# Cross attention and mixture of experts in one kernel: the first group's products, banks and splits, two context roundings moved, the slot table in two loads

## What is computed

```
x = x + (fp8(layernorm(x)) @ fp8(ctx) + mask)          # per batch, one scale for each tensor
n = layernorm(x)
scores = sigmoid(n @ router_w.T)                       # best 3 of 8 groups, best 4 experts of those
slots: 160 per expert, filled in token order           # more are dropped
routed = (silu(Xp @ W_gate) * (Xp @ W_up)) @ W_down * weight, added to its token's row
shared = silu(n @ shared_gate.T) * (n @ shared_up.T) @ shared_down.T
out = x + routed + shared
```

## Time and profile before

| | us |
|---|---|
| median of 3 runs | 1987.12 (1985.38 to 1987.95) |
| profiled execution | 1987.5 |
| its span | 1985.9 |
| PE / DVE / ACT / POOL busy | 1831.9 / 1390.6 / 864.7 / 606.0 |
| mean granted clock of PE | 0.991 |

### The profile page before, as it was taken

How to read it: one execution, slowest core, us unless ns; L and a number is a source line. 1 busy time by engine, 2 the same in 40 slices (tenths; PEclk the granted TensorE clock), 3 DMA queues, 4 the chain that set the end, 5 groups by cost and what they waited for, 6 DMA issues and landing times.

```text
span 1985.9 us, 44057 instructions
## 1 busy us (share of the span) xinstructions
PE 1831.9 (92%) x17396; PEld 1398.4 (70%) x17396; DVE 1390.6 (70%) x2509; ACT 864.7 (44%) x1209; POOL 606.0 (31%) x611
## 2 busy tenths in 40 slices
PE   0039999999999999999999999999999999999997
PEld 0018578668667767766866876778888888888886
DVE  5888675576567557557545544588888888888884
ACT  8564221222212212122221121367777777777773
POOL 2100210220220221122022022355655656656552
PEclk9989999999999999999999999999999999999999
DMA  9936534433433443434243244499999999999993
GB/s 377 392 98 198 127 86 96 109 95 86 107 98 75 107 118 68 114 96 95 76 107 75 54 107 125 140 333 356 354 370 356 355 371 354 359 372 349 363 371 78
DMA packets 188301, 395.45 MB, mean 199 GB/s; under 512 B 116304, under 2 KB 120432, under 8 KB 163600
## 3 DMA queue, kind: packets, MB, share of 16 engines
q1 hardware_dynamic: 163184, 334.77, 49.0%
q0 software_dynamic: 23808, 58.81, 13.5%
q10 hardware_dynamic: 1184, 0.15, 0.0%
HBM read 314.79 MB, written 55.35 MB: 186 GB/s over the span
## 4 chain that ended last, share of the span: by engine, by line
PE 84%; issue 3%; DVE 2%; DMA 1%; POOL 1%; SPq 0%; ACT 0%; POOLq 0%; DVEq 0%; ACTq 0%
PE ps L1345 51%; PE ps L1358 15%; PE ps L1531 8%; PE ps L1385 5%; PE ps L1539 2%; PE ps L1421 1%; DVE W L1024 1%; PE ps L1451 1%; DMA xn_rows<-FR 1%; POOL slots L555 1%; DMA FR<-xn_rows,gix 0%; PE ps L1426 0%; PE ps L1457 0%; DMA BIG<-in_sh_down 0%; SPq L467 0%
## 5 line engine op out<-in xcount | busy, mean ns | idle before, releaser
L1345 PE MATMUL ps<-XT,W 128*128 128x256 f16 (+1 forms) x12288 | 1112.4, 253 | 5.0 <-issue 2.5
L1345 PEld LDWEIGHTS ps<-XT,W 128*128 128x128 f16 x12288 | 1025.0, 98 | 90.2 <-issue 15.4
L1289 DVE SCALAR_TENSOR_TENSOR W<-BIG,W 128x2048 f16<-128x2048 f32 x192 | 436.2, 2286 | 64.5 <-ACT W L848 64.5
L848 ACT ACTIVATE W<-BIG 128x2048 f16<-128x2048 f32 x192 | 361.4, 1901 | 0.0
L1358 PE MATMUL ps<-W,HH 128*128 128x512 f16 x1536 | 334.3, 379 | 0.0
L790 ACT ACTIVATE SG<-ps 128x256 f32<-128x256 f32 x128 | 48.9, 382 | 612.5 <-PE ps L1345 612.5
L1358 PEld LDWEIGHTS ps<-W,HH 128*128 128x128 f16 x1536 | 150.3, 98 | 180.8
L257 POOL TENSOR_TENSOR expo<-expo 128x1 f32<-128x1 f32 x159 | 82.1, 516 | 621.2 <-ACT FR L719 267.4
L1203 DVE SCALAR_TENSOR_TENSOR SG<-ps,SG 128x256 f32<-128x256 f32 x128 | 54.3, 424 | 232.7 <-ACT SG L790 232.7
L548 POOL TENSOR_TENSOR rs<-ve,expo 128x1 f32<-128x1 f32 x32 | 17.6, 549 | 565.0 <-DVE ve L1045 565.0
L599 POOL DMA_INDIRECT FR<-xn_rows,gix x64 | 173.0, 2703 | 30.0 <-issue 30.0
(11 more groups left out here) (178 smaller groups left out, 1627.7 us busy)
## 6 DMA issues: line engine op xcount, KB each, us to landing
BIG<-in_w_gate SPq DMA_DIRECT2D x64, 1024.0 KB, 9.0
BIG<-in_w_up SPq DMA_DIRECT2D x64, 1024.0 KB, 7.6
BIG<-in_w_down SPq DMA_DIRECT2D x64, 1024.0 KB, 8.2
X<-in_x SPq DMA_DIRECT2D x16, 1024.0 KB, 5.2
X<-in_mask POOLq DMA_DIRECT2D x16, 1024.0 KB, 8.1
xn_rows<-FR SPq DMA_DIRECT2D x32, 512.0 KB, 3.7
out_rows<-X SPq DMA_DIRECT2D x32, 512.0 KB, 3.6
W<-in_x SPq DMA_DIRECT2D x6, 2048.0 KB, 19.6
```

What stands on the lines that cost most here:

```text
L848: ac.activation(dst, stage, ACT.Copy, scale=W_SCALE).then_inc(x_hi, 1)
L1289: ve.scalar_tensor_tensor(out=lo[cut], in0=src, scalar=W_SCALE, in1=hi[cut], op0=ALU.mult, op1=ALU.subtract).then_inc(x_lo, 1)
L1345: ins = te.matmul(out_ps, a[:, k, cols], b[:, k, :], start=n == 0, stop=n == len(steps) - 1)
```

## The change

Group 0: the products of ic 0 and 1 become `first_products`: high weights against both parts of x, in halves of 128 tokens, then the low weights piece by piece. The second tile's transposes use banks 2 and 3 and the cross product's second tile banks 6 and 7 (4 and 5 the first time). DVE makes all low splits after the x transposes; the splits get two lists, one for ACT, one for DVE, the latter after h. The router's steps on DVE come one ic later. The down pieces have four stage buffers. Two context roundings move from the end of group 0 to ic 0 and 2 of group 1. The slot table is loaded for two experts, then for the rest. In the last expert the tail rows come first and are scattered by themselves, then each half. The diff, cut to its core (some indentation removed):

```diff
@@ -157,7 +158,7 @@
 sw_stage = [W[:, 32768 + 4096 * s:32768 + 4096 * (s + 1)].bitcast(F32) for s in range(4)]
-sd_stage = [BIG[:, 10240 + 2048 * s:10240 + 2048 * (s + 1)].bitcast(F32) for s in range(3)]
+sd_stage = [BIG[:, at:at + 2048].bitcast(F32) for at in (10240, 12288, 14336, 20480)]
@@ -280,7 +283,8 @@ orders of the splits
 SW_PIECES += [(2, k, 2, nh) for nh in range(2) for k in (0, 2, 4, 6)]
-FIRST_SPLITS = [(4, 5), (6,), (7,), (8,), (9,), (10,), (11, 12), (13, 14), (15,)]
+FIRST_HI = [(4, 5), (6,), (7,), (8, 9), (10,), (11,), (), (), (12, 13, 14, 15)]
+FIRST_LO = [(4,), (5,), (6, 7), (), (), (), (), (8, 9, 10, 11), (12, 13), (14, 15)]
@@ -303,11 +307,20 @@
 def sw_slot(n):
-  return (n % 4, sw_stage[n % 4]) if n < 8 else (4 + (n - 8) % 3, sd_stage[(n - 8) % 3])
+  return (n % 4, sw_stage[n % 4]) if n < 8 else (4 + n % 4, sd_stage[n % 4])
 def sw_uses(n):
-  return n // 4 + 1 if n < 8 else (n - 8) // 3 + 1
+  return n // 4 + 1 if n < 8 else (n - 8) // 4 + 1
+def xt_bank(j, h):
+  return PS[(2 if j else 6) + h][:, :]
+def cross_bank(f, j, h):
+  first = isinstance(f, int) and f == 0
+  return PS[(2, 4 if first else 6)[j] + h][:, :]
@@ -346,11 +359,11 @@ SP sw_load
       wait(sp, sw_lo, n - 3)
-    elif n < 11:
-      wait(sp, d_cq, n - 6)
+    elif n < 12:
+      wait(sp, d_cq, n - 6 if n < 11 else 7)
     else:
-      wait(sp, sw_lo, n - 2)
+      wait(sp, sw_lo, n - 3)
@@ -380,7 +393,7 @@
     sw_load(n)
-  for n in range(4, 11):
+  for n in range(4, 12):
@@ -413,13 +426,14 @@ SP group
     if first:
-      sw_load(11)
-      sw_load(12)
...
       xq_transposes(1)
-      for n in range(13, 16):
+      for n in range(12, 16):
...
       xn_stores_and_transposes(1)
+    if isinstance(g, int) and g == 1:
+      sp.wait_ge(d_cq, 10)
+      ctx_load(11, 1)
@@ -428,7 +442,7 @@
       xq_transposes(g + 1)
-    if ctx == 2:
+    if ctx == 2 and not first:
@@ -462,9 +476,10 @@ SP
     slots = slot_dram.rearrange("(e s) w -> s e w", e=E)
-    sp.dma_start(tab[:, :, 0, :], slots[0:P]).then_inc(ld_tab, 16)
-    for c in range(TQ):
-      sp.dma_start(tab[c * TC:(c + 1) * TC, :, 1, :], slots[P:C]).then_inc(ld_tab, 16)
+    for cut, loaded in ((slice(0, 2), ld_tab), (slice(2, E), ld_tab_rest)):
+      sp.dma_start(tab[:, cut, 0, :], slots[0:P, cut]).then_inc(loaded, 16)
+      for c in range(TQ):
+        sp.dma_start(tab[c * TC:(c + 1) * TC, cut, 1, :], slots[P:C, cut]).then_inc(loaded, 16)
@@ -580,12 +595,15 @@ POOL
   main = lambda view: view.rearrange("p (e u) -> p e u", u=2)[:, :, 0]
-  ch.link(gp.tensor_scalar(tok[:, :], tab[:, :, 1, 0], float(T - 1), None, ALU.min))
-  ch.do(gp.tensor_scalar(main(gidx[:, :]), tab[:, :, 0, 0], float(T - 1), None, ALU.min))
-  ch.do(gp.tensor_scalar(tail(gidx[:, :]), tok[:, :], float(TQ), quarter[:, 0:1], ALU.mult, ALU.add))
-  ch.sync()
+  def gather_indices(cut):
+    ch.link(gp.tensor_scalar(tok[:, cut], tab[:, cut, 1, 0], float(T - 1), None, ALU.min))
+    ch.do(gp.tensor_scalar(main(gidx[:, :])[:, cut], tab[:, cut, 0, 0], float(T - 1), None, ALU.min))
+    ch.do(gp.tensor_scalar(tail(gidx[:, :])[:, cut], tok[:, cut], float(TQ), quarter[:, 0:1], ALU.mult, ALU.add))
+    ch.sync()
+  gather_indices(slice(0, 2))
   ch.close()
-  GATHER_STEPS, SLOT_STEPS = ch.before, ch.before + 4
+  GATHER_STEPS, SLOT_STEPS = ch.before, ch.before + 7
@@ -618,6 +636,8 @@
   ch.before += 1
+  pool.wait_ge(ld_tab_rest, 16 * (1 + TQ))
+  gather_indices(slice(2, E))
@@ -655,9 +675,26 @@ POOL, the last expert
   expert(E - 2, 0, more=False)
-  expert(E - 1, 1, more=False)
-  for b in range(2):
-    pool.wait_ge(st_y[b], 16 * E)
+  def last_expert(steps, carries):
+    gp.tensor_scalar(last_ix[:, 0:1], tab[:, E - 1, 0, 0:1], 2.0, None, ALU.mult).then_inc(pool_step, 1)
+    gp.tensor_scalar(last_ix[:, 1:2], tab[:, E - 1, 0, 0:1], 2.0, 1.0, ALU.mult, ALU.add).then_inc(pool_step, 1)
+    gp.tensor_copy(last_ix[:, 2:3], sidx[:, 2 * E - 1:2 * E]).then_inc(pool_step, 1)
+    pool.wait_ge(pool_step, steps + 3)
+    pool.wait_ge(st_y[0], 16 * E)
+    for n, (src, dst, u) in enumerate(((ytail[1], out_quarters, 2), (ybuf[1][:, 0:HALF], out_halves, 0),
+                     (ybuf[1][:, HALF:D], out_halves, 1))):
+      pool.wait_ge(x_y, 3 * E - 2 + n)
+      pool_carry(carries + n)
+      gp.indirect_dma_start(out=dst[:, :],
+                 out_offset=bass.IndirectOffsetOnAxis(ap=last_ix[:, u:u + 1], axis=0),
+                 in_=src, in_offset=None, bounds_check=dst.shape[0] - 1,
+                 oob_is_err=True, compute_op=ALU.add).then_inc(st_y[1], 16)
+  last_expert(SLOT_STEPS + 2 * E - 1, 4 * (E - 2) + 2 * GROUPS + 4)
+  pool.wait_ge(st_y[0], 16 * E)
+  pool.wait_ge(st_y[1], 16 * E + 16)
@@ -746,7 +783,7 @@
         ac.activation(xT[0][:, 4 * h:4 * h + 4, j * P:(j + 1) * P],
-               PS[6 + h][:, :].rearrange("p (k t) -> p k t", k=4), ACT.Copy,
+               xt_bank(j, h).rearrange("p (k t) -> p k t", k=4), ACT.Copy,
@@ -782,7 +819,7 @@ ACT group
       if first:
-        for n in FIRST_SPLITS[ic]:
+        for n in FIRST_HI[ic]:
@@ -804,6 +841,8 @@
           x_scaled(g + 1, 1 - r)
+        if isinstance(g, int) and g == 1:
+          ring_scaled(0, 32)
@@ -813,13 +852,11 @@
     if first:
-      for n in FIRST_SPLITS[KS]:
+      for n in FIRST_HI[KS]:
...
       xn_hi(g + 1)
-    if first:
-      ring_scaled(0, 32)
@@ -862,13 +899,14 @@ ACT rows_out
     act.wait_ge(st_out[b], 16 * GROUPS)
-  def rows_out(e, b, u):
+  def rows_out(e, b, u, turn=None):
     settle(act)
-    if u == 0:
+    turn = u if turn is None else turn
+    if turn == 0:
       wait(act, st_y[b], (e - b) * 16)
-    act.wait_ge(x_dn, e * 3 + (u + 1))
+    act.wait_ge(x_dn, e * 3 + (turn + 1))
@@ -1031,8 +1069,7 @@ DVE add_cross
       dve.wait_ge(pe_xa, 4 * f + 2 * j + h + 1)
-      bank = PS[4 + h] if j and isinstance(f, int) and f == 0 else PS[2 + h]
-      ve.scalar_tensor_tensor(out=at, in0=bank[:, :], scalar=sc1[:, 9:10], in1=at,
+      ve.scalar_tensor_tensor(out=at, in0=cross_bank(f, j, h), scalar=sc1[:, 9:10], in1=at,
@@ -1054,16 +1091,11 @@
                 op1=ALU.subtract).then_inc(d_lo, 1)
-  def residual(f, b):
...
...
       ve.scalar_tensor_tensor(out=xT[1][:, 4 * h:4 * h + 4, j * P:(j + 1) * P],
-                  in0=PS[6 + h][:, :].rearrange("p (k t) -> p k t", k=4), scalar=X_SCALE,
+                  in0=xt_bank(j, h).rearrange("p (k t) -> p k t", k=4), scalar=X_SCALE,
@@ -1073,11 +1105,9 @@ DVE, before the groups
   shift(0, 1)
-  split_lo(0)
-  split_lo(1)
...
   xt_lo(0, 1)
-  for n in range(2, 4):
+  for n in range(4):
@@ -1194,9 +1224,6 @@ DVE group
     for ic in range(KS):
-      if first:
-        for n in FIRST_SPLITS[ic]:
-          split_lo(n)
@@ -1206,16 +1233,22 @@
       ve.tensor_tensor(h32[ic % 2], gup, bank[:, 0:G], ALU.mult).then_inc(d_h, 1)
-      if ic == 1:
+      if first:
+        for piece in FIRST_LO[ic]:
+          split_lo(piece)
+      if isinstance(g, int) and g == 1 and ic in (0, 2):
+        ctx_round(1, 9 + ic // 2, 1 - ic // 2, 10 + ic // 2)
+      if ic - first == 1:
         route_groups(g)
-      if ic == 2:
+      if ic - first == 2:
         route_experts()
-      if ic == (5 if front else 2):
+      if ic - first == (5 if front else 2):
         route_picks()
-      if ic == (5 if front else 3):
+      if ic - first == (5 if front else 3):
         route_weights()
-      if front and ic in (3, 4):
-        x_round(g + 1, ic - 3, M_main)
+      if front and ic - first in (3, 4):
+        x_round(g + 1, ic - first - 3, M_main)
@@ -1227,12 +1260,14 @@
     if front:
-      residual(g + 1, 1 - r)
+      for j in range(NT):
+        add_cross(g + 1, 1 - r, j)
+        if first:
+          for piece in FIRST_LO[KS + j]:
+            split_lo(piece)
+        ln2_stats(g + 1, 1 - r, j)
...
         shift(g + 1, j)
-    if first:
-      for n in FIRST_SPLITS[KS]:
-        split_lo(n)
@@ -1254,16 +1289,10 @@
     add_shared(g, r, 2)
-    if first:
-      dve.wait_ge(d_cq, 9)
-      ctx_round(0, 9, 1, 10)
...
     add_shared(g, r, 3)
-    if first:
-      dve.wait_ge(d_cq, 10)
-      ctx_round(0, 10, 0, 11)
@@ -1378,11 +1407,9 @@ PE cross
       for h in range(2):
-        if j:
-          pe.wait_ge(d_x2, 4 * f + h + 1)
...
           ctx_at = (batch & 1) * (8 * D) + (k * D + h * HALF)
-          ins = te.matmul(PS[2 + h][:, :], xqT[:, k, j * P:(j + 1) * P], BIG[:, bass.ds(ctx_at, HALF)],
+          ins = te.matmul(cross_bank(f, j, h), xqT[:, k, j * P:(j + 1) * P], BIG[:, bass.ds(ctx_at, HALF)],
@@ -1394,7 +1421,7 @@ PE cross_first
         for h in range(2):
-          ins = te.matmul(PS[2 + 2 * j + h][:, :], xqT[:, k, j * P:(j + 1) * P],
+          ins = te.matmul(cross_bank(0, j, h), xqT[:, k, j * P:(j + 1) * P],
@@ -1407,9 +1434,9 @@ PE xt_transpose
       else:
-        pe.wait_ge(d_xl, 4 * f + h + 1)
+        pe.wait_ge(d_x2, h + 1)
       for k in range(4):
-        ins = te.transpose(PS[6 + h][:, k * P:(k + 1) * P], xn[j][:, (4 * h + k) * P:(4 * h + k + 1) * P],
```

(62 more changed lines are left out.)

20 lines of the change are left out of this document (7 added, 13 removed).

## The result

The changed kernel took 1991.13 us (median of 12 runs; the kernel before beside it 1987.56, also 12): a ratio of 1.0017, 95% interval 1.0009 to 1.0024. It is slower, by less than the 0.2% that the prediction took as the least it could tell. One run of the changed kernel (8953.57 us, at a granted clock of 0.214) was disturbed and is in no ratio. The profiled execution took 1990.96, its span 1989.3 against 1985.9.

What follows compares the result with a forecast made beforehand. TensorE (PE) was busy 92% of the span; group 0 was paced by SP's queue, then ACT, then DVE. Terms +2.6 - 0.6 - 0.8 = +1.2 on 1987.12 gave 1988.3 us, range 1983.0 to 1992.3.

Steps and rivals of the forecast that it cites:

- Group 0: Start of group 1 moves from 232.69 to 235.3: +2.6 us, bounds -1.5 and +6.
- First products: Group 0, ic 0 and 1: products start at 145.1, done near 158.6; PE's lead is not kept.
- (c): Clock: half speed at later 2 us gaps, 1991.9, chance 0.06; last part: earlier cold start saves up to 2 us.
- The stores: Group 0, normed rows behind 8.4 MB of transfers: land at 172.3 against 169.1, holding ACT's x scaling.
- rival (b): Slower, the stores decide: landing at 175.5 adds 3.2 more, +4.4 in all, 1991.5; chance 0.14.
- DVE's chain: Group 0: 7.8 us more DVE work, 4 us of waits gone; last shift at 220.5, 5.1 later.
- a 2 us wait: Second down product of group 0: PE waits 2 us for split 15, which comes at about 218.
- Own banks: Group 0's cross product: saves the 4.75 us wait and 1.8 us half clock, but PE meets later DVE; elsewhere 0.
- Slot table: First gather: main rows asked for 0.9 us earlier, tail rows not at all; -0.6 us, bounds 0 and -2.3.
- Last expert: End of kernel: three scatters, the last ending at 1978.9 with less data left; -0.8 us, bounds -1.5 and +0.5.
- (a): Early products carry through: stores land by 169, group 1 at 232; -4.5 us, 1982.6; chance 0.15.
- (d): The change doesn't do what it says: waits on banks stay, 4.75 and 4.42 us; chance 0.02.

Runs made afterwards that it cites:

- run 2: Changed kernel with SP issuing the two stores of group 0's normed rows ahead of weight load 4: 1986.88 us, ratio 0.9992.
- run 3: Kernel before the change, with the two stores of group 0's normed rows issued ahead of weight load 4: 1987.12 us, ratio 0.9993.
- run 7: Changed kernel with normed-row stores first, down-weight splits spread (12 in ic 6, 13 in ic 7), loads 12 and 13 ahead of SP's transposes: 1984.97 us, ratio 0.9984.
- run 5: Kernel before with slot table in two loads, changed last expert and 32 unread transposes at the start of PE's program: 1985.12 us, ratio 0.9986.
- run 10: Changed kernel with only ACT's high splits 4 and 5 moved behind the copy of the logits: 1997.94 us, ratio 1.0046.
- run 9: Kernel of run 7 with ACT's high splits 4 and 5 moved behind the copy of the logits: 1982.39 us, ratio 0.9967.
- run 4: Changed kernel with the splits of the down weights spread over the inner blocks: 1999.08 us, ratio 1.0052.
- run 6: Kernel before with only the own banks for transposes and cross product, and their waits: 1986.04 us, ratio 0.9986.
- run 8: Kernel before with both ends (table, last expert), own banks and normed-row stores first; no early products, splits as before: 1978.76 us, ratio 0.9954.
- run 11: Changed kernel with 32 unread transposes at the start of PE's program: 1990.93 us, ratio 1.0009.

## Why the prediction was right, and where it was not

It said 1988.3 and no change beyond 0.2%; 1991.13 is within the range, and +0.17% within the 0.2%, though the interval leaves no doubt of the sign. Group 0 was the dearest term, as forecast, but the sum was too low by 2.4 us (1.2 forecast, 3.57 by the medians). Two costs were missing, 2.3 us in group 0 and 1.5 in the loop, and both ends gave more than allowed, 1.4 together. That the errors partly cancel is luck.

**First products.** Transposes and start (142.81 and 144.71) as forecast, the end 2.4 us early (156.2, not 158.6): the 2.7 us charged for a cold start were 0.8 (64 half-width products in 4.49, against 3.66), so 1.9 of the up to 2 us that the last part of (c) allowed were saved. The lead was worth nothing, as forecast; ic 2 came at 164.0, not 162.1, as ACT's split 5 waited for its load as well.

**The stores** landed on the forecast: x scaling at 172.54, forecast 172.3; h of ic 2 at 177.9, forecast 177.7; ic 5 at 185.63, forecast 185.4. Runs 2 and 3 show that they were on the path: moved, they bring group 1 3.2 to 3.5 us forward. So rival (b) was right that the stores pace group 0; they only came no later than in the sum. PE's idle time before ic 4 was 1.92 and not 5 us, since it started ic 2 later and ran it at half clock at first (12.00 us for 96 products, against 10.64).

**DVE's chain** held too: split 15 done at 218.7 (forecast about 218), last shift at 221.0 (220.5), the second add ended at 230.7, 0.6 late. By the sum that add decides the start of group 1.

**The step that was off** is the price of the down product's wait: "a 2 us wait", with no clock in the sum. The cross product ended 2.3 us earlier than before, so PE met split 15 with 3.79 us of idleness, and the clock fell: 2.99 us more for 72 products (18.65 for 15.66). That made PE the later of the two paths; DVE's third add waited 1.63 us for it. At full clock PE would have waited for the second add instead, and group 1 would have started near 235.9 (230.7 and a product of 5.2; an estimate from these rows). So of the 2.3 us that were missing 1.4 are the clock's, 0.6 the chain's, and 0.3 come of the changed trace's earlier start. Run 7 takes the late splits away: 20.88 us for 96, no wait.

It is rival (c) at one place. The 2.31 us wait that was held against it did not settle it: full clock followed 1.92 us here, 2.04 in run 5 and 2.31 before, but half clock followed 2.01, 2.02 and 2.17 us (runs 10, 9 and 4). Whether the forecast wait of 2 us would have cost the clock stays open.

**Own banks: right for the changed kernel, where nothing is left of them; wrong as a price in general.** In the changed kernel PE only met split 15 earlier for them. Alone (run 6) they bring group 1 forward by 1.5 us; in run 8, with the stores first, it comes 6.2 earlier.

**Two context roundings in group 1**: 0, as forecast; PE has no wait in that group.

**Nothing was charged to groups 1 to 15**, and 1.5 us arose there. Between the logits products of neighbouring groups lie 71.14 us, and in the three stretches with a back edge 2.80 us more in all before, 4.32 after. All six kernels with the early products have 3.88 to 5.06 there, the six without 2.42 to 2.80, whatever the chip; 32 idle instructions raise it to 3.50 in the one (run 5) and lower it to 2.35 in the other (run 11). The Trainium skill (Runtime: NRT & Kernel Launch, Instruction fetch mechanics) says that code is refilled in blocks of 16 KiB, and that a taken branch out of the blocks at hand has to fetch its target. The instruction queue on the page of the profile fits (89 packets, 1.46 MB, 16.4 KB each), and so does run 11; the Trainium skill's page also calls the crossing of a block in straight code mostly hidden, which the last group of run 11 (1.31 us of gaps) does not bear out, if that is what they are. That the place of PE's instructions matters is shown, that it is the fetch is not.

**Slot table**: POOL's index operations ran as forecast, two of three 2.37 us long and ending with DVE's splits, and the main rows were asked for 0.9 us earlier, counted from the group's start. The second gather's writing ended no earlier, as forecast (46.3 us behind the logits products in both), yet its rows landed 1.2 us sooner, and the wait shrank by that and not by 0.6. Why they came faster no run shows. In run 11 the same operation fell where DVE had no split under way:

```profile
1282.58 0.24 POOL L599 TENSOR_SCALAR tok<-tab 128x2 f32<-128x2 f32 x1 [5.01 <-DMA tab<-slots]
```

0.24 us in place of 2.37. The rule of the Trainium skill that the prediction drew on (SBUF — State Buffer), an exclusive lock held for the whole instruction, agrees with both rows.

**Last expert**: the forecast charged 1.0 us of gap for each carry. The carry starts beside the descriptor writing of the scatter before it (1978.28 within 1977.17 to 1978.79), and from the end of one scatter to the start of the next 0.39 us pass. The last scatter ends at 1982.72, or 1977.8 with the 4.94 us of delay at expert 0 taken off, where 1978.9 was forecast. That is 1.0 of the 1.6 us; the rest is that only 6.6 us lie behind it in the span, where 7.1 did before.

Of the rivals, (a) did not come: PE's lead ended in ACT's waits for late loads and for the stores. (d) is out: the waits on banks are gone.
